# Last feed-forward of a four-layer network: ranked by batch, whole rows in the slots, results scattered into the output

## The reference, cut to what matters

```python
n = layernorm(x)                          # h, per token
probs = softmax(n @ gate_w + gate_b)      # 8 experts
e = argmax(probs);  p = max(probs)
rank = number of tokens up to this one that chose e
kept = rank <= 640                        # 1.25 * 4096 / 8
y = relu(n @ w1[e] + b1[e]) @ w2[e] + b2[e]
out = x + nan_to_num(p * y) if kept else x
```

## Time and profile before

| | us |
|---|---|
| median of 3 runs | 2901.34 |
| lowest and highest | 2893.95, 2903.79 |
| the profiled execution's own time | 2886.79 |
| its span, first to last instruction | 2885.1 |
| last feed-forward, in the span | 2617.9 to 2885.1 |

### The profile page before, as it was taken

How to read it: one execution, slowest core, us unless ns; L and a number is a source line. 1 busy time by engine, 2 the same in 40 slices (tenths; PEclk the granted TensorE clock), 3 DMA queues, 4 the chain that set the end, 5 groups by cost and what they waited for, 6 DMA issues and landing times. The chain is left out here.

```text
span 2885.1 us, 51402 instructions
## 1 busy us (share of the span) xinstructions
PE 2420.8 (84%) x16365; PEld 1648.7 (57%) x16365; DVE 1880.0 (65%) x3656; ACT 1462.9 (51%) x2514; POOL 1324.0 (46%) x918
## 2 busy tenths in 40 slices
PE   4478896754799999999999999999999999995190
PEld 3256663543566666666666666666666666664070
DVE  3757764676577686776776867768768677674115
ACT  1124453332465666656656666566576665663030
POOL 0214472000254745646546456456465574561524
PEclk8587897866799999999999999999999999996595
DMA  2022110013112111021121120111211201111134
GB/s 108 1 45 49 45 45 9 2 43 88 46 42 53 33 41 47 17 53 33 41 53 33 41 53 18 46 33 41 53 34 41 53 18 45 33 41 45 59 104 64
DMA packets 83150, 126.10 MB, mean 44 GB/s; under 512 B 15296, under 2 KB 58816, under 8 KB 82928
## 3 DMA queue, kind: packets, MB, share of 16 engines
q1 hardware_dynamic: 72368, 110.46, 15.4%
q0 software_dynamic: 4816, 12.13, 2.0%
q10 hardware_dynamic: 5904, 2.71, 0.3%
HBM read 57.62 MB, written 16.00 MB: 26 GB/s over the span
## 5 line engine op out<-in xcount | busy, mean ns | idle before, releaser
L2397 ACT ACTIVATE a_PT<-PS 128x512 f32<-128x512 f32 (+1 forms) x1111 | 617.6, 586 | 413.6 <-PE PS L2269 316.6
L2127 POOL TENSOR_TENSOR a_KT<-a_PT 128x512 f32<-128x512 f32 (+2 forms) x179 | 418.9, 2357 | 592.8 <-ACT a_PT L2397 592.0
L2127 POOL TENSOR_TENSOR a_KT<-a_KT,a_PT 128x2048 f32<-128x2048 f32 (+3 forms) x128 | 391.6, 3060 | 7.5
L2466 DVE TENSOR_REDUCE a_NM<-PS 128x2 fp32r<-128x512 f32 x460 | 292.4, 685 | 105.7 <-PE PS L2219 100.2
L2268 PE MATMUL PS<-a_QH,a_K 128*128 128x512 f32 (+3 forms) x768 | 313.5, 415 | 0.0
L2268 PE MATMUL PS<-a_QH,a_KSW 128*128 128x256 f32 (+2 forms) x848 | 310.5, 385 | 0.0
L2480 DVE TENSOR_REDUCE a_MX<-PS 128x1 f32<-128x512 f32 (+3 forms) x432 | 264.1, 664 | 39.5 <-PE PS L2233 25.0
L2269 PE MATMUL PS<-a_QL,a_K1B 76*128 76x512 f32 (+3 forms) x768 | 261.9, 347 | 0.0
L2230 PE MATMUL PS<-a_K,a_QH 128*128 128x512 f32 (+3 forms) x768 | 245.4, 391 | 0.4
L2216 PE MATMUL PS<-a_KSW,a_QH 128*128 128x512 f32 x460 | 198.9, 485 | 0.4
L2432 DVE TENSOR_TENSOR a_R<-PS,a_angles 128x512 f32<-128x512 f32 x153 | 102.3, 686 | 128.5 <-ACT a_TM L2348 127.9
(11 more groups left out here) (426 smaller groups left out, 5388.7 us busy)
## 6 DMA issues: line engine op xcount, KB each, us to landing
a_KWB<-a_KSW SPq DMA_DIRECT2D x68, 256.0 KB, 3.7
a_K1B<-a_K SPq DMA_DIRECT2D x32, 512.0 KB, 5.3
a_XC<-latents SPq DMA_DIRECT2D x17, 512.0 KB, 3.4
a_CKS<-latents SPq DMA_DIRECT2D x17, 512.0 KB, 4.5
a_CF<-latents SPq DMA_DIRECT2D x17, 448.0 KB, 4.1
c_EX<-in_experts SPq DMA_DIRECT2D x1, 4608.0 KB, 16.9
a_KSW<-a_KSW SPq DMA_DIRECT2D x17, 256.0 KB, 4.9
a_QS<-a_HI SPq DMA_DIRECT2D x32, 128.0 KB, 2.4
```

What stands on the lines that cost most here:

```text
L2127: nc.gpsimd.tensor_tensor(total, one_in, other_in, ALU.add).then_inc(s["added"], 1)
L2397: nc.scalar.activation(PT[:, to:to + width], turning(key)[:, 0:width], ACT.Exp).then_inc(s["taken"], 1)
L2466: ins = nc.vector.tensor_reduce(out, bank.rearrange("p (a n) -> p a n", a=2), AX.X, ALU.max, negate=True)
```

## The change

1. **Router by batch.** `T` is normalised in two halves (statistics of 16 tiles at once); `XA` and `XC` hold more than one batch, so no batch waits for another's buffers. Ranks are made per batch, by PE alone: `upto_tri` times the batch's one-hot, plus the row sums `RS` of earlier batches and the one-hot of earlier tiles, added up in PSUM (`ranks`). DVE's order is written out by hand. POOL scatters a batch's 8 tiles as soon as its slots are known.
2. **Rows side by side.** A row of `XA` is 258 words (1032 B): normalised token, the token itself, the index of its output row, its probability. It goes to the slot whole; the slots are filled with spare output rows and zeros by one DRAM-to-DRAM DMA of 5120 x 1032 B = 5.28 MB, which SP issues in `stage_heads` behind its first pass. The tensor `slots_in` becomes `slots`, allocated in `program`.
3. **Experts.** SP, not POOL, loads: weights of experts 0 and 1 at the start, all eight `XB` after the last scatter, later weights behind them. ACT, not DVE, copies the turned tokens. `slots_out`, the gathers and ACT's store are gone: `weigh` on DVE adds the bias, multiplies by the probability, replaces NaN and infinities and adds the token, on 5 tiles of an expert (3 and 2 for the last), and POOL scatters each tile of 128 rows straight into `out`. The output has 40 spare rows a partition for empty slots; `T` as it is on entry is stored to `out` first, by one DMA at the start of the stage, so that tokens that were not kept are there.
4. **Second attention.** `keep_clock`: 40 bf16 products of 384 columns that nobody reads, on PE, ahead of `tx.0.0` and again ahead of `far.0.0.0`.

There is one block instead of two, without loops. Waits that the change adds: PE's `ranks(b)` waits for the batch's one-hot and `outputs(e)` for `y_taken` of the expert before, DVE's `weigh(e)` for the scatters of expert e - 2 (`returned`), ACT's relus of e for the products of e - 2, SP's `load_weights(e)` for `y_taken` e - 1, and at the end of third attention SP waits for the fill (`emptied`).

```diff
@@ stage_attn2, tensor @@
+                def keep_clock():
+                    for _ in range(40):
+                        nc.tensor.matmul(P[7][:, 0:384], identb[:, :], masks.rearrange("p a n -> p (a n)"), start=True, stop=True)
...
+                    if st == ("tx", 0, 0) or st == ("far", 0, 0, 0):
+                        keep_clock()
@@ stage_ffn3, sync @@
+                sp.dma_start(out.rearrange("(p t) c -> p t c", p=128)[:, 0:TT, :], T[:, :, :]).then_inc(s["stored"], 16)
+                load_weights(0)
+                load_weights(1)
+                sp.wait_ge(s["scattered"], 16 * TT)
+                for e in range(E3):
+                    sp.dma_start(XB[:, e, :, :], slots[e * CAP:(e + 1) * CAP, :].rearrange("(t p) c -> p t c", p=128))\
+                        .then_inc(x_ld[e], 16)
+                for e in range(2, E3):
+                    load_weights(e)
@@ gpsimd @@
+                for b in range(B):
+                    pool.wait_ge(s["beside"], b + 1)
+                    pool.wait_ge(s["slot_ready"], b + 1)
+                    for t in range(b * NT, (b + 1) * NT):
+                        nc.gpsimd.indirect_dma_start(out=slots, out_offset=bass.IndirectOffsetOnAxis(ap=SC[:, t:t + 1], axis=0),
+                                                     in_=XA[:, t, :], in_offset=None).then_inc(s["scattered"], 16)
...
+                for e in range(E3):
+                    for t in range(CT):
+                        pool.wait_ge(s["y_done"], e * CT + t + 1)
+                        to = bass.IndirectOffsetOnAxis(ap=XB[:, e, t, IDS:IDS + 1].bitcast(U32), axis=0)
+                        nc.gpsimd.indirect_dma_start(out=out, out_offset=to, in_=YB[:, e % 2, t, :], in_offset=None)\
+                            .then_inc(returned[e], 16)
@@ tensor @@
+                for b in range(B):
+                    turn_batch(b)
+                    if b == B - 1:
+                        ranks(0)
+                    logits(b)
+                for b in range(1, B):
+                    ranks(b)
+                pe.wait_ge(s["slot_ready"], B)
+                turn_tokens(0)
+                for e in range(E3):
+                    hidden(e)
+                    if e + 1 < E3:
+                        turn_tokens(e + 1)
+                    outputs(e)
@@ scalar @@
+                for b in range(B):
+                    for h in range(2):
+                        act.wait_ge(s["xt_ready"], b * 2 + h + 1)
...
+                        nc.scalar.activation(XC[:, b % 2, h * HALF:(h + 1) * HALF], P[h], ACT.Copy).then_inc(s["xc_ready"], 1)
+                    if b > 1:
+                        exponentials(b - 2)
@@ vector @@
+                def weigh(e):
...
+                    if e > 1:
+                        dve.wait_ge(returned[e - 2], 16 * CT)
...
+                    parts = ((0, 3), (3, CT)) if e == E3 - 1 else ((0, CT),)
+                    for t0, t1 in parts:
...
+                statistics(0)
+                statistics(1)
+                normalise(0)
+                normalise(1)
...
+                normalise(2)
+                shift(0)
+                normalise(3)
+                choose(0)
+                shift(1)
+                place(0)
...
@@ stage_heads, sync @@
                 one_pass(0, 0, None)
+                sp.dma_start(slots[0:SLOTS, :], d["empty_slots"]).then_inc(emptied, 16)
```

More of the change, by code:

```diff
@@ L595, in stage_attn2 @@
         tiles, count = course.tiles, course.count
-        s = {n: keep.enter_context(nc.semaphore("a2_" + n)) for n in (*count, "ld", "ready", "rows", "stat", "inverse", "scaled",
+        s = {n: keep.enter_context(nc.semaphore("a2_" + n)) for n in (*count, "ld", "ready", "stat", "inverse", "scaled",
                                                                        "spread_q0", "spread_q1", "spread_k0", "spread_k1")}
@@ L640, in _ @@
                 sp.wait_ge(s["ld"], 32)
-                sp.wait_ge(s["rows"], 32)
+                sp.wait_ge(rows_in, 32)
             @block.gpsimd
@@ L1138, with stage_ffn3 @@
 F3 = 4 * C
-def stage_ffn3(nc, keep, PS, P, T, ident, upto_tri, d, out, stored):
+SPARE = SLOTS // 128
+ROW3 = 2 * C + 2
+IDS, PROB = 2 * C, 2 * C + 1
+def stage_ffn3(nc, keep, PS, P, T, ident, upto_tri, d, slots, out):
     with ExitStack() as ctx:
@@ L1218, in _ @@
                     last.then_inc(s["lg_ready"], 1)
[L1219 to L1234, removed]
@@ new lines, in exponentials @@
+                def exponentials(b):
+                    act.wait_ge(s["shifted"], b + 1)
+                    nc.scalar.activation(A1[:, of(b), :], LG[:, of(b), :], ACT.Exp).then_inc(s["exp"], 1)
+                for h in range(2):
+                    act.wait_ge(s["var"], h + 1)
+                    half = slice(h * TT // 2, (h + 1) * TT // 2)
+                    nc.scalar.activation(deviation[:, half], va[:, half], ACT.Sqrt).then_inc(s["std"], 1)
+                    for b in (2 * h, 2 * h + 1):
+                        nc.scalar.activation(XA[:, of(b), C:2 * C], T[:, of(b), :], ACT.Copy).then_inc(s["beside"], 1)
@@ new lines, in _ @@
+                keep_tokens(0)
+                for e in range(E3):
+                    k = e % 2
+                    if e > 1:
+                        act.wait_ge(s["y_ready"], e - 1)
+                    act.wait_ge(w_ld[k], 64 * (e // 2 + 1))
+                    for j in range(4 * sub):
+                        m, c = divmod(j, sub)
+                        act.wait_ge(s["h_ready"], e * 4 * sub + j + 1)
+                        nc.scalar.activation(H[:, k, m, c * cols:(c + 1) * cols], P[2 + j % 4][:, 0:cols], ACT.Relu,
+                                             bias=B1[:, k, m:m + 1]).then_inc(s["h_done"], 1)
+                    if e + 1 < E3:
+                        keep_tokens(e + 1)
@@ L1450 @@
+                place(3)
+                dve.wait_ge(s["cl"], 1)
+                for e in range(E3):
+                    weigh(e)
 H3 = 16
```

410 lines of the change are left out of this document (196 added, 214 removed).

## The result

The changed kernel takes **2804.73 us** (median of 4 runs, 2800.98 to 2809.78); the kernel before, beside it, 2898.86 (4 runs, 2893.95 to 2903.79). The ratio is **0.9679**, 95% interval 0.9657 to 0.9702: 94 us less. The forecast was 2816.2, with a range from 2801 to 2841.

A forecast was written before the change was run, and what follows sets the result against it. The last feed-forward was taken as a chain with nothing beside it. Gains 29.3 + 0.7 + 2.9 + 51.2 + 1.0 = 85.1 us gave 2801.7 on the profiled execution's terms, forecast as 2816.2, range 2801 to 2841.

The forecast's parts named there:

- What bounds it: Last feed-forward: a chain of waits with nothing beside it, so a microsecond saved there is saved.
- Router: Start of the last feed-forward: first scatter at 2655.6 instead of 2684.95, gain 29.3 us; bounds 5 more, 6 less.
- Scatters: POOL's 32 slot scatters in the last feed-forward: POOL binds and longer rows cost nothing, gain 0.
- long row: Rival: each slot scatter of the 1032 B row takes 1.74 us, +25, total 2841; chance 0.10.
- Handover, experts: Last scatter to products, gain 0.7 us; the eight experts without ACT's store ahead of relus, gain 2.9 us.
- The end: Last feed-forward after the experts' products: 14.0 us instead of 65.2, gain 51.2; 2 more to 6 less.
- Third attention: The 5.28 MB fill costs nothing: it takes 19 us, and loads queued behind it are first read at 827.3.
- Second attention: Two bursts in PE's waits raise its clock, but DVE's maxima soon bind: gain 1 us, 6 more to 6 less.
- POOL held by DVE: Rival: DVE's tests hold every output scatter in the experts, +6 us, total 2822; chance 0.12.
- Late ranks: Rival: PE or DVE sets router batches 1 to 3 if accumulated broadcast products cost double, +8 us, 2824; chance 0.12.
- The fill on one DMA engine: Rival in third attention: the copy takes 303 us and delays SP's next loads, total 3071; fill rival's chance 0.05.
- The level: Whole kernel: 2801.7 on the profiled execution's terms, which was 14.5 under the runs' median; forecast 2816.2.

The follow-up runs named there:

- before_bursts: The kernel before with both bursts of PE products and nothing else of the change: 2888.56 us, ratio 0.9983 to the kernel before.
- no_bursts: The changed kernel without either burst of forty PE products: 2812.35 us, ratio 0.9724 to the kernel before.
- second move: Changed kernel with ranks and exponentials one batch earlier, plus statistics of the second 16 tiles behind normalising the first 16: 2797.64 us, ratio 0.9643.
- fill_x4: The changed kernel with the table of empty slots copied four times on SP's queue instead of once: 2846.95 us, ratio 0.9817 to the kernel before.

## Why the prediction was right, point by point

**What bounds it.** Right: the stage was a chain, and 81.9 of the 84.1 forecast for it came. The signs named came too (scatters 1.26 apart, the last 41.5 behind the first, outputs 9.66 apart, no new wait of PE at 827), but for the time from the last product to the end, 16.3 where 13 to 15 had been named.

**Router.** 29.3 forecast, 29.1 measured, with errors that met: ranks 0.2 shorter than priced (3.4 against 3.6) and PE's cycle 6.07, not 6.5, against a DVE stall of 2.4 in the second statistics (the row at 2628.71; 2.4 in all eleven profiles of kernels with this order), which stood among the bounds and not in the sum. First scatter: 37.7 behind the stage's start forecast, 37.9 measured.

**Scatters.** Nothing forecast, 0.4 lost; the row of 1032 B costs what one of 512 B did. The rival "long row" is out.

**Handover, experts.** 0.7 and 2.9 forecast, 0.8 and 3.6 measured (from the first hidden product to the last bias 80.3, against 83.85). An expert takes 9.66, forecast 9.75.

**The end.** 51.2 forecast, 48.9 measured. The scatters stand at 5.7, 6.9, 8.2, 9.6 and 10.8 behind the last bias; 5.7, 7.0, 8.2, 9.5 and 10.8 had been worked out. The term that was mis-sized is what follows the last one's start: 3.2 in the sum (2.2 landing, 0.2 closing, 0.8 for a held scatter), 5.5 in the profile. The landing is as priced, 2.2; the closing takes 3.2. In the trace's records 2.11 of that are one DRAIN instruction with which POOL ends the block, at 2802.08. The kernel before has it too (2.01, at 2872.46), but there it lies beside DVE's fix-up; in the changed kernel POOL works to the end.

**Third attention.** Right for the kernel, though the cover was the wrong one (the fill four times). The 8.6 us in the table are not the change's: a pass takes 114.1 to 115.6, but up to two of the sixteen, at changing places, take 120 to 121 in twelve of the fourteen profiles, before_bursts among them, which has no fill. The changed kernel's first profile has two of them, that of before none; no_bursts, which has the fill, has none either, and its stage took 1906.4.

**Second attention.** The step that failed is "DVE's maxima of 0.7 each soon bind, gain 1". I had looked at what follows the second burst and not at how long the lower clock lasts in the kernel before: 24 us from 215.5, in which PE is 85% busy. The windows view of that stretch, before and then after (where the second burst fills it up to 221.3, and PE's other work then goes on at 1.00):

```profile
215.00:239.00 24.00, 20.42 (x94) 14.38 (x94) 12.12 (x19) 6.68 (x9) 2.30 (x2) 0.51 0.40 91
```

```profile
215.00:239.00 24.00, 23.61 (x185) 16.31 (x187) 16.08 (x32) 10.39 (x16) 6.05 (x4) 1.00 0.52 117
```

The upper bound of 6 did not hold the 10. The first burst did go as told (8.3 long within 6.4 to 12.8, tokens turned 1.2 later, counted from the stage's start), and by itself it gains nothing. The sum took the two bursts one by one; the runs show that they work only together.

**Rivals.** "POOL held by DVE" has its mechanism (1.62 us) and not its price. Its row was misread: the gather of the earlier trace rows ends 0.13 behind DVE's test, but it started, at 2867.50, beside the masked copy ahead of that test, and ends 0.85 behind that, like the scatters above:

```profile
2867.10 1.29 DVE L1445 COPY_PREDICATED f_YG<-f_bad,f_clamp 128x1024 f32<-128x1024 uint32 x1
```

"Late ranks" came true in another way than named: not the recorded products, which are as priced, but the signal behind them, 5 us on two of three chips; its 8 us had been drawn from double product cost. The fill on one DMA engine, 303 us, is out: it landed in 20.0.

**The level.** 2816.2 is 11.5 above the median. It rested on the profiled execution of before being 14.5 us under its median. In the profiles the sum errs the other way: 80.1 of span came instead of 85.1, with 9 more from the bursts, 2 less from the last feed-forward and 12 less in stages that the change does not touch or that the fill does not slow (3.6 and 8.6). So that the total came this near is in part luck: errors of both signs met, each as large as the runs of one kernel scatter (9 to 10 us). That the last feed-forward came within 2.2 us of its sum is less so: its one larger error, 2.3 at the end, was not made good elsewhere, but inside the router a stall of 2.4 and a faster cycle met.

## What to carry to other kernels

Price a lower clock by how long it lasts behind a wait, not by the instructions next to the wait, and where fillers stand in several waits, measure them together as well as one by one. Behind a long transfer on a queue look for the first thing that its issuing engine still has to send in the present pass, not only for the loads already behind it. When one engine has become the bound from its first instruction on, look at what still stands ahead of that instruction: moves of independent steps made the stage another 7 us shorter, and 11 with the second move. And compare stages of a profile on one chip: a delay of 5 us that only some chips showed looked like an effect of the edit. Where an engine goes on late, look for the semaphore's own record before blaming that engine.

## What had not been expected of the hardware

- Two bursts of PE products, each of which alone left 50 us at the lower clock, left 10 to 17 together. With the second alone the clock fell while PE was full, 4 us behind the burst's end.
- Behind four copies of 5160 KB on one queue, single issues took SP 12 to 23 us (fill_x4), where an issue takes 0.3 to 0.7.
- On two of three chips the signal of PE's products came 8 to 11 us behind their modelled end, at the same place in five profiles, while scatters were in flight; on the third 0.02 behind. DVE went on 0.02 behind the signal in each.
- All 14 scatters of POOL that took over 1 us in the changed kernel ended 0.8 us behind the end of the instruction of DVE's fix-up beside which they had started, whether it was a test, a masked copy or a multiplication.
- POOL's closing DRAIN took 2.1 us, and came at full price once POOL's work was what ended the kernel.
- Without DVE's fix-up beside them the experts were 4% slower from the fourth on, with PE's signals 1.5 us late.
